# Graph attention: the row weights R = G x exp are read from PSUM, the denominators from a small SBUF copy

## What is computed

```python
xh = (x @ W).reshape(-1, H, C)                     # H = 4 heads of C = 32
alpha = (xh[dst] * a_i).sum(-1) + (xh[src] * a_j).sum(-1)
alpha = leaky_relu(alpha, 0.2)
amax = segment_max(alpha, dst)
ex = exp(alpha - amax[dst])                        # one number per edge and head
denom = segment_sum(ex, dst)
out = segment_sum(xh[src] * (ex / denom[dst])[..., None], dst)
```

## Time and profile before

| | us |
|---|---|
| median of 3 runs (lowest to highest) | 8660.34 (8657.73 to 8661.98) |
| the profiled execution | 8661.07 |
| its span in the profile | 8659.3 |
| attention, first gather issued to last gather issued | 195.9 to 2235.1 |
| share of the span busy: GpSimd, VectorE, TensorE, ScalarE | 70%, 58%, 57%, 16% |
| TensorE clock granted in the attention stage | 0.50 of full speed |

### The profile page before, as it was taken

One profiled execution on the slowest core, in us unless ns is written; L12 is line 12 of the kernel. 1 busy time (PEld: TensorE's weight loads), 2 busy tenths in 40 slices (PEclk: granted clock), 3 DMA queues, 4 the chain that ended last, 5 costly groups with the idle time before them and its releaser, 6 DMA issues.

```text
span 8659.3 us, 148704 instructions
## 1 busy us (share of the span) xinstructions
PE 4952.0 (57%) x27078; PEld 4216.4 (49%) x27079; DVE 5035.3 (58%) x26803; ACT 1412.8 (16%) x5406; POOL 6049.8 (70%) x6331
## 2 busy tenths in 40 slices
PE   2778788787654455445455554454455545544556
PEld 1667666676644444444444444444444444444445
DVE  4777777777655555555545555555555555555555
ACT  1333333333410000000030000000003000000002
POOL 1777777777367777777737777777773777777774
PEclk7555555555555555555565555555556555555555
DMA  2444444444244444444434444444443444444443
GB/s 77 126 127 128 127 128 127 127 128 127 84 131 130 129 129 130 129 129 130 130 102 127 129 130 130 129 129 130 129 119 110 130 130 129 130 129 129 129 130 93
DMA packets 752117, 1075.13 MB, mean 124 GB/s; under 512 B 323329, under 2 KB 550727, under 8 KB 751531
## 3 DMA queue, kind: packets, MB, share of 16 engines
q0 software_dynamic: 301056, 822.48, 33.0%
q1 hardware_dynamic: 444492, 246.95, 11.3%
q10 hardware_dynamic: 6275, 3.20, 0.1%
HBM read 1027.49 MB, written 44.53 MB: 124 GB/s over the span
## 4 chain that ended last, share of the span: by engine, by line
POOL 46%; issue 23%; DMA 11%; DVE 7%; PE 7%; SPq 2%; DVEq 1%; POOLq 1%; ACT 1%; ACTq 0%
POOL G L594 46%; DMA G<-mp_rows,idx 7%; DMA G<-gat_rows,idx 2%; DVE junk L1376 2%; PE ps L1577 2%; PE ps L1672 1%; PE ps L1537 1%; SPq L534 1%; SPq L527 1%; DMA gat_rows<-ring 1%; DMA mp_rows<-acc 1%; PE ps L1574 0%; SPq L425 0%; PE ps L1564 0%; PE ps L1648 0%
## 5 line engine op out<-in xcount | busy, mean ns | idle before, releaser
L594 POOL DMA_INDIRECT G<-mp_rows,idx x4704 | 4448.6, 946 | 1807.6 <-issue 1323.1
L1672 PE MATMUL ps<-selw,G 128*128 128x32 f32 x9408 | 2222.3, 400 | 596.4 <-DVE selw L1385 595.6
L1672 PEld LDWEIGHTS ps<-selw,G 128*128 128x128 f32 x9408 | 2093.9, 328 | 878.5 <-issue 760.7
L1365 DVE TENSOR_TENSOR pen<-ps,G 128x512 f32<-128x512 f32 x1176 | 812.7, 691 | 2728.2 <-DMA G<-mp_rows,idx 2724.5
L1662 PE MATMUL ps<-awin,ring 96*128 96x128 bf16 x4704 | 715.1, 307 | 2387.0 <-DVE ring L1350 2387.0
L594 POOL DMA_INDIRECT G<-gat_rows,idx x1568 | 1561.7, 996 | 552.6 <-issue 530.7
L1662 PEld LDWEIGHTS ps<-awin,ring 96*128 96x128 bf16 x4704 | 410.1, 132 | 2540.6 <-DVE ring L1350 2540.6
L802 ACT ACTIVATE gate<-logit,cur 128x4 f32<-128x4 f32 x1176 | 349.6, 297 | 5395.0 <-DVE junk L1376 5363.0
L1376 DVE SCALAR_TENSOR_TENSOR junk<-pen,ps 128x128 f32<-128x128 f32 x4704 | 1060.3, 278 | 0.1
L1350 DVE TENSOR_TENSOR ring<-ring,ps 96x512 bf16<-96x512 bf16 x1176 | 795.6, 677 | 0.4
L1577 PE MATMUL ps<-sel,weighted 128*128 128x32 f32 x3136 | 750.8, 404 | 0.0
(11 more groups left out here) (182 smaller groups left out, 5074.3 us busy)
## 6 DMA issues: line engine op xcount, KB each, us to landing
ring<-rel_dst SPq DMA_DIRECT2D x1176, 96.0 KB
G<-mp_rows,idx POOLq DMA_INDIRECT x4704
ring<-rel_dst SPq DMA_DIRECT2D x392, 128.0 KB
awin<-mp_dst_rows SPq DMA_DIRECT2D x1176, 24.0 KB
G<-gat_rows,idx POOLq DMA_INDIRECT x1568
mp_rows<-acc SPq DMA_DIRECT2D x30, 625.0 KB
mp_dst_rows<-acc SPq DMA_DIRECT2D x30, 468.8 KB
sm<-gat_si SPq DMA_DIRECT2D x392, 0.5 KB
```

Of the source, the lines that this page charges most:

```text
L594: pool.indirect_dma_start(out=G[:, u, width * t:width * (t + 1)], out_offset=None, in_=table, in_offset=bass.IndirectOffsetOnAxis(ap=idx[: ...
L1365: v.tensor_tensor(pen[:, off % 2, :].rearrange("p (t c) -> p t c", t=T), PS[off % 2][:, :].rearrange("p (t c) -> p t c", t=T), Grows[:, of ...
L1672: i = mm(PS[2 + off % 2][:, 0:W], Grows[:, off % U, t, 0:D], selw[:, off % 4, W * t:W * t + W], start=(t == 0), stop=(t == T - 1))
```

## The change

`gat_exp` writes the 128x512 exponentials to a whole PSUM bank (6 or 7) instead of to SBUF, and `gat_R` reads them there. A second, small activation of the same input writes 128x16 exponentials to a new SBUF tile `ex4`, from which `gat_den` now takes its weights. Banks 6 and 7 are no longer free for the denominators, so these go to columns 64 to 95 of bank 4 or 5, the bank that also takes the numerators. For this TensorE's wait for `tt` of two groups before moves from `gat_nd` to `gat_den`, ahead of it, and takes the place of the wait for `den4`. `gat_al0` waits for `ex4` instead of `ex`, since `ex4` is the last reader of `al`.

```diff
-        ex = weighted[:, 2:4, :]
+        ex4 = sb("ex4", [P, 2, T * H])
...
                 act.wait_ge(done["den"], k0 + (off + 1))
-                nc.scalar.copy(den4[:, off % 2, :], PS[6 + off % 2][0:H, 0:W]).then_inc(done["den4"], 1)
+                nc.scalar.copy(den4[:, off % 2, :], PS[4 + off % 2][0:H, 2 * W:3 * W]).then_inc(done["den4"], 1)
...
                 act.wait_ge(done["al"][3], k0 + (off + 1))
-                nc.scalar.activation(ex[:, off % 2, :].rearrange("p (s c) -> p s c", c=C),
+                nc.scalar.activation(PS[6 + off % 2][:, :].rearrange("p (s c) -> p s c", c=C),
                                      al[:, off % 2, 3, :].unsqueeze(2).to_broadcast([P, T * H, C]),
                                      ACT.Exp).then_inc(done["ex"], 1)
+                nc.scalar.activation(ex4[:, off % 2, :], al[:, off % 2, 3, :], ACT.Exp).then_inc(done["ex4"], 1)
...
                 if reached(k0, off, 2, done):
-                    dve.wait_ge(done["ex"], k0 + (off - 1))
+                    dve.wait_ge(done["ex4"], k0 + (off - 1))
                 v.tensor_tensor(a[:, 0, :, :], e[:, :, 0:H], Grows[:, off % U, :, D:D + H],
...
                 v.tensor_tensor(R[:, off % 2, :].rearrange("p (t c) -> p t c", t=T), Grows[:, off % U, :, 0:D],
-                                ex[:, off % 2, :].rearrange("p (t c) -> p t c", t=T), ALU.mult).then_inc(done["R"], 1)
+                                PS[6 + off % 2][:, :].rearrange("p (t c) -> p t c", t=T), ALU.mult).then_inc(done["R"], 1)
...
                 if reached(k0, off, 2, done):
-                    pe.wait_ge(done["den4"], k0 + (off - 1))
+                    pe.wait_ge(done["tt"], 2 * k0 + (2 * off - 2))
                 pe.wait_ge(done["sel"], k0 + (off + 1))
-                pe.wait_ge(done["ex"], k0 + (off + 1))
+                pe.wait_ge(done["ex4"], k0 + (off + 1))
                 for t in range(T):
-                    i = mm(PS[6 + b][0:H, 0:W], ex[:, b, D * t:D * t + D:C], sel[:, off % U, W * t:W * t + W],
+                    i = mm(PS[4 + b][0:H, 2 * W:3 * W], ex4[:, b, H * t:H * t + H], sel[:, off % U, W * t:W * t + W],
                            start=(t == 0), stop=(t == T - 1))
                 i.then_inc(done["den"], 1)
...
             def gat_nd(k0, off, done=gat):
                 b = off % 2
-                if reached(k0, off, 2, done):
-                    pe.wait_ge(done["tt"], 2 * k0 + (2 * off - 2))
                 pe.wait_ge(done["den4"], k0 + (off + 1))
```

More of the change, by code:

```diff
@@ L297, in gnn_kernel @@
         gat_sems = {name: sem(f"gat_{name}") for name in (
-                    "selT sel pen sjT mx dg mxs ma hi r1 mid r2 e8s den den4 rhs e8 mnew dd mkept ex "
+                    "selT sel pen sjT mx dg mxs ma hi r1 mid r2 e8s den den4 rhs e8 mnew dd mkept ex ex4 "
                     "ee R nd tt acc").split()}
```

## The result

The changed kernel takes 8593.78 us (median of 6 runs, 8592.92 to 8596.18), the kernel before 8661.16 in the same comparison: a ratio of 0.9922, 95% interval 0.9909 to 0.9935. 67 us are gone, where 66 were forecast.

The account below looks back on a forecast made before the run. GpSimd's attention gathers were taken as the bound: 78.4 us of surplus less 12 of remaining collisions and 0.3 for the drain gives 66.1 us, so 8595.0 (8594.3 for the median); 8 in 10 between 8579 and 8635.

Parts of the forecast that it names:

- What bounds: Attention stage: lasts as long as its GpSimd gathers, one behind the other, 1,568 x (0.996 + 0.305) = 2,040 us.
- Edit 1: R's second input in PSUM: removes 71.0 us of gather surplus in the attention stage, R itself unchanged.
- Edit 2: Attention gathers still lengthened by VectorE instructions other than R: 12 us left, between 7 and 20, against 7.4 before.
- chance placement: Collision estimate: an instruction of length d lengthens a gather by (d - 0.126) squared over twice 1.251 us on average.
- Edits 3 and 4: ScalarE's exponentials, large into PSUM 0.63 us, small into ex4 0.2 us, covered by 3.1 us idle a group.
- Edit 5: TensorE's tt wait ahead of the denominators: 0 to 0.6 us a turn, e8 0.1 us later at the standstill, hidden.
- What is late next: VectorE-TensorE loop in attention: 38.8 us a turn of eight groups, 1.2 under the gathers' 40.0, which stay the bound.
- The third rival: Slower: the VectorE-TensorE loop becomes the bound, from 0.15 us a group on; 8793 us, chance 5%.
- The sum: Attention stage 78.4 - 12 = 66.4 us less, drain takes back 0.3, leaving 66.1.
- the drain: End of the attention stage, where no gather covers the new wait: takes back some 0.3 us.
- Other collisions move in: Rival: gathers and VectorE fall in step, L987 or L983 hit most times; gain 27 us, 8633, chance 7%.
- The change doesn't do what it says: Rival: surplus belongs to L1052 and L1055 behind R, or the port is held otherwise; 8655 to 8665, chance 6%.

Follow-up runs that it names:

- e1: Changed kernel with the 128x512 exponentials and R's second input back in SBUF, all else kept: 8696.8 us, 1.0019 of the kernel before.
- m1b: Changed kernel plus an unused 128x512 VectorE product, both inputs in SBUF, per message-passing group behind L1366: 8788.8 us, 1.0145 of the kernel before.
- m2b: Changed kernel plus an unused 128x512 VectorE product, second input in PSUM, per message-passing group behind L1366: 8602.4 us, 0.9931 of the kernel before.
- m5: Changed kernel plus an unused 128x512 product, both inputs in SBUF, ending VectorE's step in message passing: 8915.0 us, 1.0292 of the kernel before.
- e2: Changed kernel with ScalarE's small exponential writing 128x512 numbers to SBUF instead of 128x16: 8613.2 us, 0.9922 of the kernel before.
- e8: Not a run: TensorE work in the attention stage (L1549 before, L1550 in the changed kernel), queued behind den and nd; VectorE waits for it at L1063.
- e3: Changed kernel plus one unused VectorE product per attention group, one input in PSUM: 8615.3 us with 128x128, 8614.8 with 128x512, both 0.9925.
- e4: Changed kernel plus two unused 128x512 VectorE products per attention group, one input of each in PSUM: 8790.8 us, 1.0148 of the kernel before.
- m1: Changed kernel plus an unused 128x512 product, both inputs in SBUF, per message-passing group: 10,783 us where the kernel before took 10,704.7.
- m4: Changed kernel plus an unused 128x128 product, both inputs in SBUF, per message-passing group: 10,858 us where the kernel before took 10,704.7.
- m2: Changed kernel plus an unused 128x512 product, second input in PSUM, per message-passing group: 10,878 us where the kernel before took 10,704.7.

## Why the prediction was right

**What bounds.** Right: the stage lasted as long as its gathers before and after, with 0.3 us between them, and the gain is the sum of what they got shorter.

**Edit 1, R's input.** Right in kind and size: 71.0 us forecast and gone (none of 167 gathers held up); e1 brings them back, and m1b against m2b shows the same of another product on other data. R's own duration as forecast (685 ns against 691).

**Edit 2, the collisions that stay.** Forecast 12 us (7 to 20), measured 11.6. The value was good by luck as well, since it stood between a row of before and chance placement, and m1b and m5 (171 and 315 us where chance gives 149) show how far placement can be from chance.

**Edits 3 and 4, ScalarE.** 600 ns (forecast 630, bounds 590 and 720) and 199 (forecast 200). Covered, as e2 shows with twice the dose. One step was wrong: I had den4 and the index copy behind it come 4.5 us later at the standstill, and over 5 us left between index and gather. The smallest distance is 10.0 us, as good as the 10.2 before (the loop's first group, with 9.8 us before and after, set aside in both). ScalarE's mask (L681), which stands ahead of den4, waits for selT and so for the end of VectorE's standstill anyway; the new wait of TensorE delays den4 hardly beyond that:

```profile
1416.62 0.72 ACT L681 ACTIVATE pen<-ring,negbig 128x512 f32<-128x512 bf16 x1 [7.37 <-DVE ring L988]
```

**Edit 5, the wait for tt.** Right that it stays hidden; the terms were off. In the steady steps nothing is lost, where I kept 0 and 0.07 us. At the standstill TensorE starts 0.25 us after tt and not at once, so e8 comes 0.3 to 0.4 us later and not 0.1 (rhs would have let it start near 1418.8; it starts at 1419.21). By an estimate from these lengths that would be 15 to 20 us over 49 turns, had VectorE and TensorE been the bound. What I didn't see is that the edits other than R's input shift VectorE against the gathers: with R's input in SBUF they cost 16.5 us (e1). Whether this edit or the added exponential does it is open.

**What is late next.** Wrong in the working, right in what followed from it. I took 38.8 us a turn by adding lengths; the two engines overlap, and e3 showed the reserve to be not 0.15 us of VectorE time a group but at least 0.6. The third rival was therefore further off than I had it. The point from which it decides lies between one and two products of 128x512 (e3, e4).

**The sum.** The stage: 67.4 us less (2039.2 to 1971.8 from first to last gather), forecast 66.4. 0.3 for the drain was too small: between the last gather of the stage and the first of message passing lie 153.8 us, 2.3 more than before. It isn't R's input, for e1 has the same 153.8 (and e2, m1b, m2b and m5 153.6 to 153.9); which of the other edits it is stays open. That the total, 67.4 us less by the medians, came so near 66.1 is partly luck: message passing, which the change doesn't touch, took 1.7 us less in the profiled execution.

**The rivals.** "Other collisions move in" did not happen in the changed kernel (L984 and L988 hold up 106 of 1,568 gathers, with 6.3 us), but it is real: in m1 576 gathers were caught by a product that began 50 to 80 ns behind their start, VectorE having fallen in step with them. "The change doesn't do what it says" is out: L1053 and L1056 follow R in the changed kernel as L1052 and L1055 did before, and the surplus is gone; and the product of m1b has no such instructions behind it, and holds gathers up by the same rule.

## What to carry to other kernels

Where GpSimd makes the descriptors of gathers and is the bound, look at what VectorE runs when a gather starts: a long instruction with two SBUF inputs, or a fast one with one, adds what is left of its length, less some 0.13 us, to the gather, and putting one input in PSUM takes that away at no cost in the instruction. Such a price is a matter of placement, so read it off the timeline (end of gather less end of instruction is constant) and not off a mean, and expect any other edit that moves VectorE's instants to change it. Two engines that hand work to each other overlap: reckon the pace as the larger of the two, and test the reserve by adding work.

## What the runs showed of the hardware beyond that

- The moment that counts isn't simply the gather's start. Products that began 0 to 50 ns after it held nothing up in m1 (15 gathers, 950 ns at most), 568 of the 575 that began 60 to 80 ns after it did:

```profile
3500.24 1.57 POOL L594 DMA_INDIRECT G<-mp_rows,idx  x1 [0.30 <-issue]
3500.30 0.68 DVE L1369 TENSOR_TENSOR weighted<-rel_all 128x512 f32<-128x512 f32 x1
```

  (3500.30 + 0.68 + 0.82 = 3501.80, and 3500.24 + 1.57 = 3501.81.) From 80 ns on there was again nothing. In m5, with another instruction ahead of the product, all 144 products that began 0 to 160 ns after a gather's start held it up. Nor does a product that began just before the gather always count: in m4 none of the 78 that began up to 34 ns before it did, in m5 the same distance was enough. Where the edges lie, and what the instruction before has to do with it, stays open; the prediction's "0.126 us after its start" is a fit, good for instructions that begin well before the gather.
- The gather holds VectorE up as well. L987, the fast one-input instruction, took 341 to 385 ns in the kernel before where no gather was under way at its start. Where it began 0.48 to 0.67 us into a gather, 107 took more than 20 ns over the median of 347, up to 584, and all of these ended 1.06 to 1.07 us after the gather's start. R, with two SBUF inputs and the usual pace, took 677 to 694 ns wherever it began.
- A gather of message passing took 945.7 ns on average in some executions and 948.5 in others, on one chip and with the same instructions there (e4 and e2); over 6,272 gathers that is 18 us. It is the size of the step between the 8,661 us and the 8,680 us of the kernel before, though no trace of that kernel at 8,680 us was kept. Why the length changes no run shows. Two kernels are compared safely only side by side.
- Where the kernel before took 10,705 us, the attention gathers of m2 stretched over 3,002 us at 86 GB/s, though each took GpSimd its usual 949 ns. Data landed later, and GpSimd waited for indices and buffers that depend on it. What delayed it no run shows.
